# Layer-norm, K evacuation and filler work moved between engines in an attention and mixture-of-experts kernel on eight cores

## The reference

```python
x = x + attn(layernorm(x), W, b)          # q, k, v = x W + b; softmax(q k^T / 32, causal) v
x = x + moe(layernorm(x), router_w, w1, w2, shared_gate_up, shared_down, shared_gate_w)
```

## Time and profile before

| what | us |
|---|---|
| median of two timed runs | 2648.62 |
| the two runs | 2565.88 and 2731.37 |
| the profiled execution's own time | 2559.84 |
| its span (slowest core, core 6) | 2558.3 |
| spans of the eight cores | 2540.4 to 2558.3 |
| PE busy in the span | 2143.6 (84%) |
| DVE busy | 811.4 (32%) |
| ACT busy | 637.4 (25%) |

### The profile page before, as it was taken

How to read it: one execution, slowest core, us unless ns; L and a number is a source line. 1 busy time by engine, 2 the same in 40 slices (tenths; PEclk the granted TensorE clock), 3 DMA queues, 4 the chain that set the end, 5 groups by cost and what they waited for, 6 DMA issues and landing times.

```text
span 2558.3 us, 26320 instructions; the slowest of 8 cores (2540.4 to 2558.3 us)
## 1 busy us (share of the span) xinstructions
PE 2143.6 (84%) x9600; PEld 931.7 (36%) x9600; DVE 811.4 (32%) x1009; ACT 637.4 (25%) x1192; POOL 60.4 (2%) x190
## 2 busy tenths in 40 slices
PE   1436999989899898978771666899999999999999
PEld 0112343334333333333320222444444444444444
DVE  3424434444544444454442111303122130211203
ACT  4202331431523414252324222020211102011120
POOL 0000000000000000000000000000000000000000
PEclk8777999999999999989885778999999999999999
DMA  7462421430522314243313333003322222322023
GB/s 156 100 87 79 85 46 33 93 87 5 118 50 64 99 30 96 56 91 70 81 38 60 50 50 49 1 1 50 49 34 34 34 33 44 55 34 34 1 33 132
DMA packets 204064, 149.73 MB, mean 59 GB/s; under 512 B 176160, under 2 KB 176288, under 8 KB 203936
## 3 DMA queue, kind: packets, MB, share of 16 engines
q1 hardware_dynamic: 189872, 101.88, 16.9%
q0 software_dynamic: 14064, 46.16, 12.0%
HBM read 142.79 MB, written 8.39 MB: 59 GB/s over the span
## 4 chain that ended last, share of the span: by engine, by line
PE 69%; DMA 8%; ACT 8%; DVE 5%; SPq 3%; issue 2%; ACTq 2%; DVEq 2%
PE pO L897 17%; PE sp L876 17%; PE pO L505 9%; PE pO L536 9%; DMA xb<-xkv 4%; PE pO L417 4%; PE sp L796 3%; PE sp L801 3%; PE sp L348 3%; SPq L226 3%; DMA xb<-xq 3%; ACTq L51 2%; PE pO L263 2%; PE pO L846 2%; DVEq L51 2%
## 5 line engine op out<-in xcount | busy, mean ns | idle before, releaser
L876 PE MATMUL sp<-Q_sb,w 128*128 128x512 bf16 x2048 | 443.3, 379 | 0.0
L897 PE MATMUL pO<-w_sb,hb 128*128 128x512 bf16 x2048 | 443.3, 379 | 0.0
L906 DVE SCALAR_TENSOR_TENSOR O<-pO,c_sb,O 128x1024 f32<-128x1024 f32 x128 | 164.3, 1284 | 719.7 <-PE pO L897 719.7
L417 PE MATMUL pO<-V_sb,PTd 128*128 128x512 bf16 x1088 | 268.7, 404 | 66.8 <-DMA PTd<-P 63.5
L884 ACT ACTIVATE hb<-sp 128x1024 bf16<-128x1024 f32 x128 | 131.3, 1026 | 752.7 <-PE sp L876 752.7
L348 PE MATMUL sp<-K_sb,Q_sb 128*128 128x512 bf16 x1088 | 256.3, 391 | 52.1 <-ACT P L390 38.5
L876 PEld LDWEIGHTS sp<-Q_sb,w 128*128 128x128 bf16 x2048 | 200.4, 98 | 241.6
L897 PEld LDWEIGHTS pO<-w_sb,hb 128*128 128x128 bf16 x2048 | 200.4, 98 | 241.6
L505 PE MATMUL pO<-xlnT,wkv_sb 128*128 128x512 bf16 x1024 | 226.6, 384 | 59.4 <-DMA xlnT<-xlnb 59.4
L536 PE MATMUL pO<-wkv_sb,xlnT 128*128 128x512 bf16 x1024 | 232.0, 380 | 0.5 <-DVE V_sb L549 0.5
L796 PE MATMUL sp<-Q_sb,wgu 128*128 128x512 bf16 x256 | 113.0, 441 | 103.9 <-DVE hb L815 80.2
(11 more groups left out here) (81 smaller groups left out, 1040.6 us busy)
## 6 DMA issues: line engine op xcount, KB each, us to landing
xb<-xkv SPq DMA_DIRECT2D x64, 512.0 KB, 5.1
xb<-xq SPq DMA_DIRECT2D x32, 512.0 KB, 4.8
w<-w1p POOLq DMA_DIRECT2D x8, 2048.0 KB, 16.9
w_sb<-w2p POOLq DMA_DIRECT2D x8, 2048.0 KB, 16.8
out<-O SPq DMA_DIRECT2D x16, 512.0 KB, 2.6
wkv_sb<-wkvh POOLq DMA_DIRECT2D x2, 2048.0 KB, 32.2
wgu<-wguh POOLq DMA_DIRECT2D x16, 256.0 KB, 6.3
wq_sb<-wqh POOLq DMA_DIRECT2D x1, 2048.0 KB, 22.1
```

Source lines behind the costliest of these rows:

```text
L417: p.emit("tensor", lambda e, i=i, nb2_=nb2_, t=t, rr=rr, f=(i == 0), l=(i == nchunk - 1): e.matmul(pO[t % 2][:, nb2_ * 512:nb2_ * 512 + 51 ...
L876: p.emit("tensor", lambda e, e_i=e_i, th=th, fc=fc, dc=dc, nbq=nbq, jj=jj: e.matmul(sp[jj][:, nbq * 512:nbq * 512 + 512], w1_sb[e_i % 2][: ...
L897: p.emit("tensor", lambda e, th=th, tc=tc, fc=fc, nbq=nbq: e.matmul(pO[tc % 2][:, nbq * 512:nbq * 512 + 512], hb[th][:, fc * 1024 + tc * 1 ...
L906: p.emit("vector", lambda e, tl=tl, tc=tc, e_i=e_i: e.scalar_tensor_tensor(out=O[tl][:], in0=pO[tc % 2][:], scalar=c_sb[:, tl * 8 + e_i: t ...
```

## The change

Three edits. In the first phase the normalisation of odd chains is done on ACT (line 213) instead of DVE; even chains stay on DVE. The eight evacuations of each K projection move from DVE to ACT as an `Identity` activation with the bias, and the first QK of a block waits for that. The fixed number of filler items in an iteration goes from 3 to 4. All lines after 303 are one higher in the changed kernel.

```diff
-            ev_ln = ln_back(key, lambda xbs=xbs: xb[xbs][:], norm_eng="V")
+            ev_ln = ln_back(key, lambda xbs=xbs: xb[xbs][:],
+                            norm_eng="V" if (i - 1) % 2 == 0 else "SC")
...
-    kprojst = {"v": 0}
+    kprojst = {"sc": 0}
...
-            p.wait("vector", T, T.n)
-            p.emit("vector", lambda e, kc=kc, rot=rot: e.tensor_scalar(
-                out=K_sb[:, kc * 1024:kc * 1024 + 1024], in0=pO[rot][:],
-                scalar1=bksb[:, kc:kc + 1], scalar2=None, op0=ALU.add), inc=V)
-            pO_free_v[rot] = V.n
+            p.wait("scalar", T, T.n)
+            p.emit("scalar", lambda e, kc=kc, rot=rot: e.activation(
+                out=K_sb[:, kc * 1024:kc * 1024 + 1024], in_=pO[rot][:],
+                func=AF.Identity, bias=bksb[:, kc:kc + 1]), inc=SC)
+            pO_free_sc[rot] = SC.n
...
-        kprojst["v"] = V.n
+        kprojst["sc"] = SC.n
...
-        p.wait("tensor", V, kprojst["v"])
+        p.wait("tensor", SC, kprojst["sc"])
...
-            npop = max(3, -(-kv_left // iters_left)) if iters_left > 0 else 3
+            npop = max(4, -(-kv_left // iters_left)) if iters_left > 0 else 4
```

## The result

The kernel before takes 2567.71 us in the median of 10 runs, the changed kernel 2618.63 us in the median of 11; the ratio is 1.0205, 95% interval 1.0189 to 1.0222. The two profiled executions, 2559.84 and 2616.77, differ by 56.9 us in the time and in the span.

A forecast was written before the change was run, and what follows sets the result against it. How long filler items hold the softmax tile loop, through in-order queues, was taken to bound the kernel, not DVE or ACT load. 63.2 - 6 - 1.2 = +56.0 on 2559.84 gave 2616 us; range 2588 to 2645.

The forecast's parts named there:

- The base: Whole kernel: the sum is counted from the profiled execution's 2559.84 us, not from the shown median of 2648.62.
- The clock, the term put at nothing: AVs after longer gaps, five blocks: 0 to 18 us, none taken; as rival +18, 2634 and more, 20%.
- Part 1, item count: Blocks 0 to 6: four filler items per iteration instead of three put the tiles back, 63.2 us slower.
- Blocks 5 to 7: Blocks 5 and 6: the second `p3` load now stands before the last `PTd<-P`, 3 us each.
- The reading behind it: Block 5, already with four items: SP holds three key transposes before tile 4's `PTd<-P`; exponential 5 no earlier than +46.8.
- The rival that the items would end sooner without slowing the loop: Blocks 0 to 4: idle shrinks with fewer item-carrying iterations, 2540 us, if exponential 5 begins by +41.3; chance 8%.
- Only the key items cost: Rival, tile loop: the second `p3` load is hidden, 37 - 7 = +30 us, 2590; chance 14%.
- Part 2, first phase: First phase: odd normalisations on ACT free chains 9 and 17 from waiting behind query evacuations on DVE, -6 us.
- Part 3: K evacuation on ACT: QK's wait for the last one shortens in 7 blocks, -1.2 us, bounds -1.2 to 0.

The follow-up runs named there:

- held transposes: Changed kernel, with SP issuing an iteration's item transposes behind the next `PTd<-P`, or ahead of the normalisation overwriting their buffer: 2538.84 to 2545.82 us.

## Why the number was right and two steps of the prediction failed

The sum was +56.0 on the profiled 2559.84; the profiles differ by 56.9, and the compared runs by 2.05% against the 2.2% forecast. The measured 2618.63 lies in the range. Two steps failed all the same.

- *The base.* Against the one median that was shown, 2648.62, a time of 2616 is a kernel 1.2% faster, and the whole range lies below it; the kernel became 2.05% slower. The prediction set that median aside, counted from the profiled execution and never said what its number meant against it. The further runs bear its choice out: six of the ten runs of the kernel before lie between 2558.96 and 2567.78. So the number can be read as right only beside 2560 to 2568, not beside the median on the table.
- *The clock, the term put at nothing.* "I take none" was said of 0 to 18 us, for the reason that part of it would fall into waits. But in the windows of blocks 0 to 5 PE's busy time, which holds no waits, is 337.7 us against 322.4, 15.3 more, with matmul counts that differ by one at most. These windows are 62.8 us longer together; the other 47.5 are idle, where the sum had 60.2 for the same six blocks. The order on SP was read rightly, but its chain was put 12.7 us too long and the clock 15.3 too short. That the sum is within 1 us is the luck of two errors of opposite sign.

The interval, 1.0189 to 1.0222, lies across the 2% bound, so "slower by over 2%" is more likely than not but not settled.

- *Part 1, item count.* Forecast 63.2 over seven blocks, measured 64.0 in the two profiles, 67 in the mean of the cores, and 55 to 71 alone in runs. By block 0 to 4, forecast and measured: 6.2 and 9.0, 13.9 and 12.3, 12.0 and 11.7, 13.2 and 13.1, 11.9 and 11.0. In block 0 AV(4) was put at +46.8 and came at +47.0, but took 6.40 us instead of 3.5. In block 1 the chain ran as written and each step a little shorter: exponential 6 at +58.9 (forecast +62.1), AV(6) at +68.8 (+72.0), because loads landed in 4.3 us instead of the 5.25 taken from block 5; AV(6) then took 5.16 instead of 3.5 and QK(9) came at +73.8 (+75.5).
- *Blocks 5 to 7.* Forecast 3 and 3 for blocks 5 and 6 and nothing for block 7; in the mean of the cores they cost 6.1, 5.9 and 1.9. In block 5 the two last AVs, which followed each other without a gap, now have one between them:

```profile
1169.84 6.05 PE L418 MATMUL pO<-V_sb,PTd 128*128 128x512 bf16 x16 [9.40 <-DMA PTd<-P]
1179.07 6.55 PE L418 MATMUL pO<-V_sb,PTd 128*128 128x512 bf16 x16 [3.18 <-DMA PTd<-P]
```

  The same two in the kernel before:

```profile
1123.83 9.17 PE L417 MATMUL pO<-V_sb,PTd 128*128 128x512 bf16 x32 [9.21 <-DMA PTd<-P]
```

  The gap is the 3 us forecast. But the two AVs take 12.6 us together instead of 9.17, so the clock costs as much again.
- *The reading behind it*, that the order on SP and not the time on ACT or DVE makes the loss, was a reading of block 5 when the forecast was made. The held transposes show it: the same work in another order takes 73 us off. The rival that the items would end sooner without slowing the loop had exponential 5 at +41.3 or before; it came at +45.9 in block 1. (The forecast's +46.8 was the start of the tiny instruction ahead of the exponential in block 5; the exponential itself stood at +47.4 there.) That rival's price was also read a little low: the idle time of the earlier trace rows in blocks 0 to 4 is 51 us, not 45, and in all six 66, not 70.
- *Only the key items cost*, the rival at +30: false. Exponential 6 came later by the second load, as forecast. A buffer of its own for that load gives back 12 to 16 us, and three retire items instead of four about 28. What the `Q_sb` transposes ahead of `PTd<-P` cost by themselves wasn't run apart.
- *Part 2, first phase.* Forecast -6, measured -7.5 on the two profiled cores, -6.8 in the mean of eight. Chain 17's transpose was forecast near 131 (131.27), the first K matmul to run on near 209 (208.46). With all odd chains on ACT the whole kernel gained 9 to 24 us, more than the term; with two chains 8 to 17.
- *Part 3.* Forecast -1.2, measured -2.7 in the profile: the evacuation takes 1115 ns on ACT, as taken from the nearest row, but QK also starts 0.13 us sooner behind it. The Trainium skill's rule to keep additions on VectorE ("ScalarE: Activation LUTs", Rules for kernel authors) doesn't hold for this shape: 1284 ns on DVE, 1115 on ACT. The Trainium skill gives its factor of three for bf16, and this source is fp32 in PSUM. The estimate worked out from its cost for a pointer bias ("ScalarE: Activation LUTs", What ACT_TABLE_LOAD costs) was 1133.

## What to carry to other kernels

A count of filler work per iteration isn't a matter of engine load: ask of each filler which in-order queue it stands in, what it waits for there, and what of the main loop stands behind it. Here a transpose that waits for a normalisation, and a load that waits for an add, stood ahead of the one transpose that the next matmuls needed; with the transposes issued behind it and the second load in a buffer of its own the same four items per iteration took 1% less than the kernel before instead of 2% more, and with three items it was 3% less. A stage in the trace that already runs in the mode a change proposes (here block 5, with four items) is a good measure of it. A term given a range of 0 to 18 us and then put at nothing needs a reason from the trace: here it came to 15.

## What wasn't expected

- How much the mended order gives with three items: every block stretch is 6 to 13 us shorter than before in the mean of the cores, and the run came out far below its expectation. Whether that is the first load of a block, now issued ahead of the wait for the V projection, or the order of the transposes behind it, wasn't run apart.
- How often a gap of 3 to 5 us before an AV slowed it: 12 of 13 times in blocks 0 to 6, to 5.2 to 6.6 us instead of 3.5 for its 16 matmuls. A gap as long before a QK slowed that QK in only some blocks (5.30 us after 3.25 in block 2, 3.61 after 3.23 in block 1). Leaving this out was the largest single error in block 0.
- One DMA transpose held SP for 18 to 22 us while the 4 MB of weights were loaded from POOL, in each of the fourteen profiles, whichever chain's it was.
